# Turning normalised tokens by halves, inside the stage in front, at three seams of a hybrid attention kernel

## The chip, the cores and the metric

One core of one Trainium2 chip runs the whole program. The metric is the device time of one execution in microseconds, lower being better. The profiled execution's span runs from the program's first instruction to its last.

## What is computed

For each of 16 sequences of L = 1024 tokens with D = 256 channels, float32, a block of four residual steps:

```python
x = x + attn_a(layernorm(x))     # delta rule + two causal convolutions + values, mixed by a router, then Wo
x = x + slot_ffn(layernorm(x))   # 64 slots, top-8 routing, a GRU step on the slots, values mixed back
x = x + attn_b(layernorm(x))     # causal softmax attention, 16 heads of 16
x = x + slot_ffn(layernorm(x))
def layernorm(x): return (x - mean(x)) / sqrt(var(x) + 1e-5)      # over the channels
```

The slot step begins with `h = gelu(layernorm(x) @ w1 ...)` and softmax attention with `qkv = layernorm(x) @ w_qkv`. Both need the normalised tokens with the channels on the partitions.

## The kernel before

A hardware loop goes over the 16 sequences; each is a row of stages: convolutions and delta rule, router, mixing (`mix_and_project`), slot step `ffa`, softmax attention (`softmax_attention`), slot step `ffb`. A stage is one or more Blocks. In a Block each engine has a program of its own, in the order in which it is written, and waits for others by semaphores; at a Block's end all five engines meet, and only then does the next Block begin.

The tokens live in SBUF as T = 8 tiles of 128 tokens by 256 channels (`k.x1`, normalised in `k.xn`). PSUM is `ps`, 8 banks of 512 float32 a partition. `k.xnT` holds the normalised tokens turned: 2 halves of the channels (`HALVES`) by 1024 tokens, which are 2 halves of 512 tokens (`NB`, `BANK`). So a turning is 16 transposes of 128x128 on TensorE (PE) into four banks, then two copies by ScalarE (ACT) and two by VectorE (DVE).

A seam is the end of one stage and the beginning of the next. There are three in question: mixing to `ffa` (the mixing seam), `ffa` to softmax attention (the slot seam), and softmax attention to `ffb` (the softmax seam). At each, in front of the Block's end:

- PE projects to the tokens (L1238, L1352, L1769), two tiles to a bank.
- VectorE adds them to `k.x1` and takes the statistics, two tiles at a time (L303, L266 to L272); GpSimd raises to the power -1/2 and makes the shift (L280, L282); ScalarE normalises tile by tile (L287).
- PE, done with its projection, runs 8 matmuls of `keep_warm` (L312), whose results nobody reads.

Behind the Block's end PE turns all 16 (L319), ScalarE copies (L327), VectorE copies (L333), and the next stage's first matmuls follow: L1292 in a slot step, L1804 in softmax attention. They wait for `xn0` and `xn1`, once for each half of the tokens. In the slot step L1399 is VectorE's first instruction on the router's logits; in softmax attention L1618 is the first matmul of scores for the running maximum.

The trace has two records for each float32 matmul that is not a transpose: L1292 is 4 matmuls and 8 records, L1804 16 and 32.

Of the kernel before, what the change touches and what calls it, by code (L numbers as in the profile page):

```python
# [18 lines left out]
ACT = mybir.ActivationFunctionType  # L19
# [4 lines left out]
P = 128  # L24
SEQS, L, D = 16, 1024, 256
T = L // P
HALVES = D // P
# [262 lines left out]

def normalise(nc, k, s, act, x):

    for t in range(T):
        act.wait_ge(s.rstd, 2 * (t // 2 + 1))
        normalise_tile(nc, k, x, t)

# [17 lines left out]

def turn_normed_pe(nc, k, ps, s):
    for n in range(NB):
        for a in range(HALVES):
            for i in range(BANK // P):
                last = nc.tensor.transpose(ps[:, 4 + HALVES * n + a, i * P:(i + 1) * P],  # L319
                                           k.xn[:, n * (BANK // P) + i, a * P:(a + 1) * P], k.ident[:])  # L320
            last.then_inc(s.xn_turned, 1)


def turn_normed_act(nc, k, ps, s, act):
    for n in range(NB):
        act.wait_ge(s.xn_turned, HALVES * n + 1)
        nc.scalar.activation(k.xnT[:, 0, n * BANK:(n + 1) * BANK], ps[:, 4 + HALVES * n, :], ACT.Copy).then_inc(s.xn0, 1)  # L327


def turn_normed_dve(nc, k, ps, s, dve):  # L330
    for n in range(NB):
        dve.wait_ge(s.xn_turned, HALVES * n + 2)
        nc.vector.tensor_copy(k.xnT[:, 1, n * BANK:(n + 1) * BANK], ps[:, 4 + HALVES * n + 1, :]).then_inc(s.xn1, 1)  # L333


def first_norm(nc, k, ps, s, io):

    with nc.Block() as block:
        @block.scalar
        def _(act):  # L340
            for t in range(T):
                act.wait_ge(s.rstd, 2 * (t // 2 + 1))
                normalise_tile(nc, k, k.x0, t).then_inc(s.next_normed, 1)
            turn_normed_act(nc, k, ps, s, act)

        @block.vector
        def _(dve):
            settle = chain_of(dve, s.dve)
            dve.wait_ge(io.loaded, 16)
            for u in range(T // 2):  # L350
                norm_statistics(nc, k, s, settle, k.x0, u)
            turn_normed_dve(nc, k, ps, s, dve)

        @block.gpsimd
        def _(pool):
            inverse_deviations(nc, k, s, pool)

        @block.tensor
        def _(pe):
            pe.wait_ge(s.next_normed, T)  # L360
            turn_normed_pe(nc, k, ps, s)
    clear(nc, s)
# [770 lines left out]
def mix_and_project(nc, k, m, ps, s):  # L1133

    with ExitStack() as tmp:
# [20 lines left out]
        with nc.Block() as block:  # L1156
# [8 lines left out]
            @block.vector  # L1165
            def _(dve):
                settle = chain_of(dve, s.dve)
                for n in range(NB):
                    for i in range(PATHS):
                        nc.vector.tensor_tensor(of(paths[i], n), of(paths[i], n),  # L1170
                                                m.prob[:, n * GN:(n + 1) * GN, i:i + 1].to_broadcast([P, GN, DH]),
                                                ALU.mult).then_inc(s.part, 1)
                for n in range(NB):
                    dve.wait_ge(s.summed, n + 1)
                    nc.vector.tensor_scalar(ms[:, n * GN:(n + 1) * GN], ps[:, SUMS + n, 0:GN], EPS * EPS, None,
                                            ALU.add).then_inc(s.scale_in, 1)
# [5 lines left out]
                add_with_statistics(nc, k, s, dve, settle, lambda u: ps[:, 4 + u, :], base=k.x0)  # L1182

            @block.scalar
            def _(act):
# [10 lines left out]
                normalise(nc, k, s, act, k.x1)  # L1196

            @block.tensor
            def _(pe):
# [52 lines left out]
                project(1)  # L1252
                keep_warm(nc, k, ps[:, 0, :], 8)
    clear(nc, s)
# [7 lines left out]
def slot_ffn(nc, k, ps, s, tag, io=None, store=None, load=None):  # L1262

    with ExitStack() as tmp:
# [19 lines left out]
        with nc.Block() as block:  # L1284
            @block.tensor
            def _(pe):
                turn_normed_pe(nc, k, ps, s)
                for n in range(NB):
                    pe.wait_ge(s.xn0, n + 1)
                    pe.wait_ge(s.xn1, n + 1)  # L1290
                    for c in range(HALVES):
                        last = nc.tensor.matmul(ps[:, n, :], k.w1x[:, c, :], k.xnT[:, c, n * BANK:(n + 1) * BANK],  # L1292
                                                start=(c == 0), stop=(c == HALVES - 1))
                    last.then_inc(s.h_ps, 1)
# [53 lines left out]
                for t in range(T):  # L1348
# [5 lines left out]
                    if t % 2:  # L1354
                        last.then_inc(s.out, 1)
                keep_warm(nc, k, ps[:, 7, :], 8)

            @block.scalar
            def _(act):
                turn_normed_act(nc, k, ps, s, act)  # L1360
                for n in range(NB):
# [29 lines left out]
                if store is None:  # L1391
                    normalise(nc, k, s, act, k.x1)

            @block.vector
            def _(dve):
                settle = chain_of(dve, s.dve)
                turn_normed_dve(nc, k, ps, s, dve)
                dve.wait_ge(s.logits, 1)
# [46 lines left out]
                if store is None:  # L1445
                    add_with_statistics(nc, k, s, dve, settle, lambda u: ps[:, u, :])
                else:
                    for u in range(T // 2):
# [96 lines left out]
def softmax_attention(nc, k, ps, s, stacked, ones_rows):  # L1545

    with ExitStack() as tmp:
# [231 lines left out]
        with nc.Block() as block:  # L1779
# [15 lines left out]
            def _(pe):  # L1795
                turn_normed_pe(nc, k, ps, s)
                for u in range(2 * HALVES * NB):
                    i, a, n = unit(u)
                    pe.wait_ge(s.xn0, n + 1)
                    pe.wait_ge(s.xn1, n + 1)  # L1800
                    if u >= 4:
# [53 lines left out]
                for t in range(BANK // P, T):  # L1855
                    last = project_out_pe(pe, late_slot, t, range(1, HALVES))
                    if t % 2:
                        last.then_inc(s.out, 1)
                keep_warm(nc, k, ps[:, RING_BANK, :], 8)

            @block.scalar
            def _(act):
# [3 lines left out]

                turn_normed_act(nc, k, ps, s, act)
                for u in range(2 * HALVES * NB + 1):
# [17 lines left out]
                nc.scalar.activation(oT[:, 1, BANK:L], ps[:, RING_BANK, :], ACT.Copy).then_inc(s.ot1, 1)  # L1886
                normalise(nc, k, s, act, k.x1)

            @block.vector
            def _(dve):  # L1890
                settle = chain_of(dve, s.dve)
                turn_normed_dve(nc, k, ps, s, dve)
                for u in range(2 * HALVES * NB):
# [26 lines left out]
                for u in (2, 3):  # L1920
                    add_out_dve(dve, settle, late_slot, u)
                    norm_statistics(nc, k, s, settle, k.x1, u)

            @block.sync
# [43 lines left out]

COMMON = "dve var rstd xn_turned xn0 xn1"
SET_OF = {"su": 1, "pc": 2, "dr": 1, "ro": 0, "mi": 1, "ff": 0, "sa": 1}  # L1970
# [163 lines left out]
```

## Time and profile before

| | |
|---|---|
| median of 3 runs | 8637.09 us (8602.2 to 8650.65) |
| profiled execution | 8632.0 us, its span 8630.2 us |
| granted TensorE clock, mean over the span | 0.921 |
| busy: PE, DVE, ACT, POOL | 90%, 56%, 39%, 17% |
| instructions | 126086 |

[...]

### The profile page before, as it was taken

Reading aid. Unit: us, or ns where it says so; the run is one execution under the profiler, and the core shown is the slowest. Engines: PE = TensorE matmul, PEld = TensorE weight load, DVE = VectorE, ACT = ScalarE, POOL = GpSimd, SP = SyncE. Lnnn points to the kernel's source line nnn. Section 1 sums busy time; section 2 is a strip of 40 time slices with the busy share of each in tenths; the row PEclk is TensorE's granted clock in tenths of the full one; section 3 lists DMA queues with packets and bytes.
Section 4 is the critical chain, followed back from the end, with each engine's and each line's share of the span. In section 5 each row is a group of like instructions: output and inputs, shape, how many; then the busy total and the mean of one; then the engine's idle time right before and its main releaser. Section 6 shows DMA issues by size and latency. Waiting matters only on the chain. (4 is left out here: it accounts for less than half of the span.)

```text
span 8630.2 us, 126086 instructions
## 1 busy us (share of the span) xinstructions
PE 7756.3 (90%) x49774; PEld 4709.9 (55%) x49774; DVE 4846.4 (56%) x9442; ACT 3377.0 (39%) x6843; POOL 1453.5 (17%) x2145
## 2 busy tenths in 40 slices
PE   6899998989889899898988988999899998998889
PEld 4546465464554646546465464654646546465464
DVE  5555655556645566555665546555465554656546
ACT  2252533525335243352533425334253342534425
POOL 2102121121211212112121121211212112121111
PEclk9999989989989898999989999899898999989989
DMA  2120111201112021120211102111021110211102
GB/s 70 19 41 17 31 44 23 43 10 31 44 23 43 10 31 44 23 43 10 36 40 29 38 9 36 40 31 45 1 36 40 31 45 1 41 35 31 45 1 40
DMA packets 337658, 268.92 MB, mean 31 GB/s; under 512 B 213377, under 2 KB 276225, under 8 KB 336953
## 3 DMA queue, kind: packets, MB, share of 16 engines
q1 hardware_dynamic: 337004, 260.04, 15.3%
q8 instruction: 430, 7.05, 0.4%
q14 instruction: 224, 1.84, 0.1%
HBM read 48.66 MB, written 42.02 MB: 11 GB/s over the span
## 5 line engine op out<-in xcount | busy, mean ns | idle before, releaser
L1716 ACT ACTIVATE sa_pt<-ps 128x512 f32<-128x512 f32 (+3 forms) x3072 | 1283.4, 492 | 793.7 <-PE ps L1705 639.3
L1637 DVE TENSOR_REDUCE sa_nm<-ps 128x2 f32<-128x1024 f32 (+4 forms) x1280 | 1388.9, 1115 | 341.0 <-PE ps L1618 148.3
L1701 PE MATMUL ps<-sa_qs,sa_ks 99*128 99x512 bf16 (+3 forms) x3072 | 846.3, 332 | 55.8 <-ACT sa_pt L1716 40.3
L1618 PE MATMUL ps<-sa_ks,sa_qs 96*128 96x512 bf16 (+3 forms) x2560 | 629.6, 320 | 50.8 <-DVE sa_nm L1637 32.1
L312 PE MATMUL ps<-identb 128*128 128x512 bf16 x2560 | 647.9, 405 | 10.5 <-ACT dr_z L988 10.5
L1726 PE MATMUL ps<-sa_pt,sa_va 128*17 128x512 f32 (+3 forms) x6144 | 641.8, 491 | 0.0
L1701 PEld LDWEIGHTS ps<-sa_qs,sa_ks 99*128 99x128 bf16 x3072 | 288.2, 98 | 613.3 <-ACT sa_pt L1716 411.6
L576 PE MATMUL ps<-rep,stack 128*32 128x512 f32 x4608 | 501.0, 593 | 0.0
L280 POOL TENSOR_TENSOR rstd<-vare,mhalf 128x2 f32<-128x2 f32 x260 | 181.3, 697 | 1789.8 <-DVE vare L272 1789.8
L312 PEld LDWEIGHTS ps<-identb 128*128 128x128 bf16 x2560 | 259.9, 105 | 316.7 <-issue 77.7
L287 ACT ACTIVATE xn<-x,shift,rstd 128x256 f32<-128x256 f32 x520 | 278.4, 593 | 393.8 <-POOL shift L282 393.4
L797 POOL TENSOR_TENSOR A<-paths 128x256 f32<-128x256 f32 x384 | 269.6, 734 | 866.9 <-DVE paths L954 866.9
L1705 PE MATMUL ps<-causalT,identb 128*128 128x128 bf16 x2048 | 414.3, 221 | 0.0
L678 DVE SCALAR_TENSOR_TENSOR k_tm<-pre,cw,k_tm 128x1024 f32<-128x1024 f32 x192 | 245.3, 1284 | 233.5 <-ACT k_tm L620 228.9
L1618 PEld LDWEIGHTS ps<-sa_ks,sa_qs 96*128 96x128 bf16 x2560 | 241.1, 99 | 223.1 <-DVE sa_nm L1637 61.1
L1622 PE MATMUL ps<-causal,identb 128*128 128x128 bf16 x1792 | 336.3, 220 | 0.0
L576 PEld LDWEIGHTS ps<-rep,stack 128*32 128x32 f32 x4608 | 146.5, 110 | 335.0 <-issue 335.0
L1206 PE MATMUL ps<-ident,paths 128*128 128x128 f32 x2048 | 265.8, 296 | 67.1 <-DVE paths L1170 67.1
L1068 DVE COPY ro_partial<-ps 128x512 f32<-128x512 f32 x32 | 22.1, 692 | 539.3 <-PE ps L1100 539.3
L1658 POOL CAST sa_mp<-sa_nm 128x16 bf16<-128x16 f32 x128 | 25.3, 198 | 1723.8 <-DVE sa_nm L1637 1723.8
L319 PE MATMUL ps<-ident,xn 128*128 128x128 f32 x784 | 148.6, 370 | 169.6 <-PEq L1156 54.9
L1206 PEld LDWEIGHTS ps<-ident,paths 128*128 128x128 f32 x2048 | 260.1, 211 | 68.7 <-DVE paths L1170 68.7
(343 smaller groups left out, 14866.5 us busy)
## 6 DMA issues: line engine op xcount, KB each, us to landing
sa_qs<-sa_parts SPq DMA_DIRECT2D x288, 128.0 KB, 4.4
sa_ks<-sa_parts SPq DMA_DIRECT2D x288, 128.0 KB, 5.7
x<-in_x SPq DMA_DIRECT2D x17, 1024.0 KB, 5.5
rep<-paths SPq DMA_DIRECT2D x128, 128.0 KB, 2.3
bounce<-paths SPq DMA_DIRECT2D x32, 512.0 KB, 2.6
out_y<-x SPq DMA_DIRECT2D x32, 512.0 KB, 3.0
rep<-paths SPq DMA_DIRECT2D x128, 127.9 KB, 2.4
rep<-paths SPq DMA_DIRECT2D x128, 127.8 KB, 2.3
```

Of the source, the lines that this page charges most:

```text
L287: return nc.scalar.activation(k.xn[:, t, 0:D], x[:, t, :], ACT.Identity, bias=k.shift[:, t:t + 1], scale=k.rstd[:, t:t + 1])
L312: nc.tensor.matmul(scratch, k.identb[:, 0:P], k.identb[:], start=True, stop=True)
L576: last = nc.tensor.matmul(ps[CG * g:CG * (g + 1), 4 + u % 4, :], k.stack[:, (base + j) * GROUPS + gg, :], rep[:, gg, PAD + n * BANK - SHIF ...
L797: nc.gpsimd.tensor_tensor(with_delta[:, t % 2, 1 + n, :], m.delta_tm[:, t, :], paths[n][:, t, :], ALU.mult).then_inc(s.d_products, 1)
L1206: last = nc.tensor.matmul(ps[:, HALVES * n + a, j * P:(j + 1) * P], paths[i][:, n * TN + j, a * P:(a + 1) * P], k.ident[:], start=(i == 0 ...
L1618: last = nc.tensor.matmul(cols[:, i, :], qs[0:NCOMB * AD, g % NBUF, op.j + i, op.t * P:(op.t + 1) * P], ks[0:NCOMB * AD, g % NBUF, op.j + ...
L1622: last = nc.tensor.matmul(cols[:, i, op.w - P:], k.identb[:, 0:P], k.causal[:], start=False, stop=True, skip_group_check=True)
L1637: nc.vector.tensor_reduce(nm[:, g % 2, op.c, op.t, op.j:op.j + op.heads], cols, AX.X, ALU.max, negate=True).then_inc(s.slot_free, 1)
L1701: last = nc.tensor.matmul(bank[:, off:], ks[0:QROWS, g % NBUF, j, kt * P:(kt + 1) * P], qs[0:QROWS, g % NBUF, j, n * BANK + off:(n + 1) * ...
L1705: last = nc.tensor.matmul(bank[:, off:off + P], k.identb[:, 0:P], k.causalT[:], start=False, stop=True, skip_group_check=True)
L1716: nc.scalar.activation(pt[:, gs % 2, j, off:BANK], ring_bank(ring_use(gs, j))[:, off:], ACT.Exp, scale=RATIO).then_inc(s.ring_out, 1)
L1726: last = nc.tensor.matmul(ps[2 * AD * j:2 * AD * j + AD + 1, SUM_BANK, off:BANK], va[:, kt, g * GH + j, :], pt[:, gs % 2, j, off:BANK], st ...
```

## The change

The first norm of the program, in front of the loop, is turned by the same new functions. At the three seams the turning moves in front of the Block's end and is cut in two by halves of the tokens: PE waits for tiles 0 to 3, turns them, runs warm-ups (12 in the mixing and slot seams, 10 in the softmax seam, where 8 stood), waits for tiles 4 to 7 and turns them. ScalarE copies its part of the first half behind tile 5 and that of the second behind tile 7; VectorE copies behind its last statistics. The next stage's first matmuls wait for nothing but the Block. Banks of `ps` are given by `first`: 0 to 3 in the mixing seam, 4 to 7 in the others.

```diff
-def normalise(nc, k, s, act, x):
+def normalise_and_turn(nc, k, ps, s, act, first):
     for t in range(T):
         act.wait_ge(s.rstd, 2 * (t // 2 + 1))
-        normalise_tile(nc, k, x, t)
+        normalise_tile(nc, k, k.x1, t).then_inc(s.xn_normed, 1)
+        if t in (T - 3, T - 1):
+            turned_act(nc, k, ps, s, act, first, t // (T - 1))
...
+def turn_pe(nc, k, ps, s, pe, first, n):
+
+    pe.wait_ge(s.xn_normed, (n + 1) * (BANK // P))
+    for a in range(HALVES):
+        for i in range(BANK // P):
+            last = nc.tensor.transpose(ps[:, first + HALVES * n + a, i * P:(i + 1) * P],
+                                       k.xn[:, n * (BANK // P) + i, a * P:(a + 1) * P], k.ident[:])
+        last.then_inc(s.xn_turned, 1)
+
+
+def turned_act(nc, k, ps, s, act, first, n):
+
+    act.wait_ge(s.xn_turned, HALVES * n + 1)
+    nc.scalar.activation(k.xnT[:, 0, n * BANK:(n + 1) * BANK], ps[:, first + HALVES * n, :], ACT.Copy)
+
+
+def turned_dve(nc, k, ps, s, dve, first, n):
+
+    dve.wait_ge(s.xn_turned, HALVES * n + 2)
+    nc.vector.tensor_copy(k.xnT[:, 1, n * BANK:(n + 1) * BANK], ps[:, first + HALVES * n + 1, :])
...
                 project(1)
-                keep_warm(nc, k, ps[:, 0, :], 8)
+                turn_pe(nc, k, ps, s, pe, 0, 0)
+                keep_warm(nc, k, ps[:, 2, :], 12)
+                turn_pe(nc, k, ps, s, pe, 0, 1)
...
-                turn_normed_pe(nc, k, ps, s)
                 for n in range(NB):
-                    pe.wait_ge(s.xn0, n + 1)
-                    pe.wait_ge(s.xn1, n + 1)
...
-                keep_warm(nc, k, ps[:, 7, :], 8)
+                if store is None:
+                    turn_pe(nc, k, ps, s, pe, 4, 0)
+                    keep_warm(nc, k, ps[:, 6, :], 12)
+                    turn_pe(nc, k, ps, s, pe, 4, 1)
+                else:
+                    keep_warm(nc, k, ps[:, 7, :], 8)
...
-                keep_warm(nc, k, ps[:, RING_BANK, :], 8)
+                turn_pe(nc, k, ps, s, pe, RING_BANK, 0)
+                keep_warm(nc, k, ps[:, SUM_BANK, :], 10)
+                turn_pe(nc, k, ps, s, pe, RING_BANK, 1)
```

PE's program at the mixing seam before, with line numbers of the kernel before; `mi_ot` is the mixed output that is projected, L1156 and L1285 are the end of one Block and the beginning of the next:

```order
L1238 MATMUL ps<-wo,mi_ot 128x256 x16
L312 MATMUL ps<-identb 128x512 x8
L1156 UNCONDITIONAL_BRANCH
L1285 UNCONDITIONAL_BRANCH
L319 MATMUL ps<-ident,xn 128x128 x16
L1292 MATMUL ps<-xnT,w1x 128x512 x4
```

And in the changed kernel, with its own line numbers (L1245 is the projection, L322 the turning, L314 the warm-ups, L1298 the slot step's first matmuls):

```order
L1245 MATMUL ps<-wo,mi_ot 128x256 x16
L322 MATMUL ps<-ident,xn 128x128 x8
L314 MATMUL ps<-identb 128x512 x12
L322 MATMUL ps<-ident,xn 128x128 x8
L1161 UNCONDITIONAL_BRANCH
L1294 UNCONDITIONAL_BRANCH
L1298 MATMUL ps<-xnT,w1x 128x512 x4
```

The turning stands in front of the Block's end in two pieces, with the warm-ups between them. At the slot seam PE's program in the changed kernel is this; L1358 gives the slot step's output, L1812 is softmax attention's first matmul:

```order
L1358 MATMUL ps<-ffa_values,ffa_alphat 128x256 x8
L322 MATMUL ps<-ident,xn 128x128 x8
L314 MATMUL ps<-identb 128x512 x12
L322 MATMUL ps<-ident,xn 128x128 x8
L1293 UNCONDITIONAL_BRANCH
L1805 UNCONDITIONAL_BRANCH
L1812 MATMUL ps<-xnT,wqkvT 128x512 x16
```

The last 8 transposes are queued behind all 12 warm-ups. ScalarE's program at the mixing seam in the changed kernel; L287 normalises, L330 is its copy of turned tokens, L1373 the slot step's first activation:

```order
L287 ACTIVATE xn<-x,shift,rstd 128x256 x6
L330 ACTIVATE xnT<-ps 128x512
L287 ACTIVATE xn<-x,shift,rstd 128x256 x2
L330 ACTIVATE xnT<-ps 128x512
L1161 UNCONDITIONAL_BRANCH
L1369 UNCONDITIONAL_BRANCH
L1373 ACT_TABLE_LOAD
```

Before, eight L287 stood in a row in front of the Block's end and both copies behind it; now one copy stands between the sixth and the seventh tile.

## Rows read from the trace of the kernel before

**Rows 1.** The page, first part: busy us, share of the span, instructions.

```profile
PE 7756.3 (90%) x49774; PEld 4709.9 (55%) x49774; DVE 4846.4 (56%) x9442; ACT 3377.0 (39%) x6843; POOL 1453.5 (17%) x2145
```

**Rows 2.** Waits: who waited for whom, us in total, times, longest us.

```profile
PE ps L319 <- PEq L1156: 54.9, 16, 3.4
```

**Rows 3.** Timeline, first mixing seam: start us, us, what [idle before it, its end].

```profile
328.73 1.89 PE L312 MATMUL ps<-identb 128*128 128x512 bf16 x8
328.80 1.09 ACT L287 ACTIVATE xn<-x,shift,rstd 128x256 f32<-128x256 f32 x2 [0.84 <-POOL shift L282]
...
332.66 1.09 ACT L287 ACTIVATE xn<-x,shift,rstd 128x256 f32<-128x256 f32 x2 [0.83 <-POOL shift L282]
...
334.05 3.65 PE L319 MATMUL ps<-ident,xn 128*128 128x128 f32 x16 [3.43 <-PEq L1156]
...
336.02 0.69 DVE L333 COPY xnT<-ps 128x512 f32<-128x512 f32 x1 [4.45 <-PE ps L319]
...
337.49 4.87 PE L1292 MATMUL ps<-xnT,w1x 128*128 128x512 f32 x8
...
344.28 0.69 DVE L1399 TENSOR_TENSOR ffa_lg<-ps,b 128x512 f32<-128x512 f32 x1 [5.86 <-PE ps L1297]
```

**Rows 4.** Timeline, first softmax seam.

```profile
551.17 2.06 ACT L287 ACTIVATE xn<-x,shift,rstd 128x256 f32<-128x256 f32 x4
...
554.61 2.13 PE L312 MATMUL ps<-identb 128*128 128x512 bf16 x8
...
559.58 1.94 PE L319 MATMUL ps<-ident,xn 128*128 128x128 f32 x16 [2.84 <-PEq L1779]
...
560.68 0.69 DVE L333 COPY xnT<-ps 128x512 f32<-128x512 f32 x1 [3.57 <-PE ps L319]
...
561.52 3.67 PE L1292 MATMUL ps<-xnT,w1x 128*128 128x512 f32 x8
```

**Rows 5.** Mixing seams, 16 stretches: A:B, us, busy us (instructions), PEclk, DMA.

```profile
333.75:344.28 10.53, 10.23 (x41) 7.34 (x42) 1.38 (x3) 5.04 (x7) 0.00 (x0) 0.70 0.00 0
...
8362.67:8370.50 7.83, 7.53 (x41) 5.26 (x42) 1.38 (x2) 5.04 (x7) 0.00 (x0) 1.00 0.00 0
sum 158.79, PE 154.07 PEld 112.64 DVE 22.16 ACT 80.54 POOL 0.00; mean PE 9.63 PEld 7.04 DVE 1.39 ACT 5.03 POOL 0.00
```

**Rows 6.** Slot seams, 16 stretches, columns as in rows 5.

```profile
378.32:394.54 16.22, 15.91 (x49) 7.73 (x49) 6.23 (x9) 8.49 (x16) 6.61 (x7) 1.00 0.16 54
...
8404.14:8422.43 18.29, 17.98 (x49) 9.66 (x49) 6.23 (x9) 8.49 (x16) 6.61 (x7) 0.86 0.14 48
sum 272.05, PE 267.19 PEld 135.29 DVE 99.61 ACT 135.85 POOL 105.62; mean PE 16.70 PEld 8.46 DVE 6.23 ACT 8.49 POOL 6.60
```

**Rows 7.** Softmax seams, 16 stretches, columns as in rows 5.

```profile
559.29:567.11 7.82, 7.53 (x41) 5.26 (x42) 1.39 (x2) 5.03 (x6) 0.00 (x0) 1.00 0.43 135
1093.58:1102.84 9.26, 8.97 (x41) 6.63 (x42) 1.39 (x3) 5.03 (x6) 0.00 (x0) 0.82 0.36 113
...
sum 142.03, PE 137.34 PEld 101.63 DVE 22.16 ACT 80.48 POOL 0.00; mean PE 8.58 PEld 6.35 DVE 1.38 ACT 5.03 POOL 0.00
```

**Rows 8.** Timeline, first slot seam, then the last sequence's.

```profile
366.75 6.65 PE L1352 MATMUL ps<-ffa_values,ffa_alphat 64*128 64x256 f32 x16 [0.51 <-DVE ffa_values L1444]
...
373.33 3.60 PE L312 MATMUL ps<-identb 128*128 128x512 bf16 x8
...
380.56 13.97 PE L1804 MATMUL ps<-xnT,wqkvT 128*128 128x512 f32 x32
...
8396.62 1.90 PE L312 MATMUL ps<-identb 128*128 128x512 bf16 x8
...
8404.44 3.65 PE L319 MATMUL ps<-ident,xn 128*128 128x128 f32 x16 [5.91 <-PEq L1284]
```

**Rows 9.** Stretches of the first slot seam, columns as in rows 5.

```profile
367.40:377.50 10.10, 9.53 (x23) 5.20 (x21) 7.42 (x28) 3.55 (x7) 3.57 (x8) 0.50 0.00 0
377.70:394.54 16.84, 15.91 (x49) 7.73 (x49) 6.23 (x9) 9.11 (x17) 6.61 (x7) 1.00 0.15 52
```

More of the change, by code:

```diff
@@ L312, in keep_warm @@
         nc.tensor.matmul(scratch, k.identb[:, 0:P], k.identb[:], start=True, stop=True)
[L315 to L333, printed above, removed]
+def turn_pe(nc, k, ps, s, pe, first, n):
[11 more added lines that the diff above has]
+    nc.vector.tensor_copy(k.xnT[:, 1, n * BANK:(n + 1) * BANK], ps[:, first + HALVES * n + 1, :])
 def first_norm(nc, k, ps, s, io):
@@ L342, in _ @@
                 act.wait_ge(s.rstd, 2 * (t // 2 + 1))
-                normalise_tile(nc, k, k.x0, t).then_inc(s.next_normed, 1)
-            turn_normed_act(nc, k, ps, s, act)
+                normalise_tile(nc, k, k.x0, t).then_inc(s.xn_normed, 1)
+            for n in range(NB):
+                turned_act(nc, k, ps, s, act, 4, n)
         @block.vector
@@ L351, in _ @@
                 norm_statistics(nc, k, s, settle, k.x0, u)
-            turn_normed_dve(nc, k, ps, s, dve)
+            for n in range(NB):
+                turned_dve(nc, k, ps, s, dve, 4, n)
         @block.gpsimd
@@ L359, in _ @@
         def _(pe):
-            pe.wait_ge(s.next_normed, T)
-            turn_normed_pe(nc, k, ps, s)
+            for n in range(NB):
+                turn_pe(nc, k, ps, s, pe, 4, n)
     clear(nc, s)
@@ L1182, in _ @@
                 add_with_statistics(nc, k, s, dve, settle, lambda u: ps[:, 4 + u, :], base=k.x0)
+                for n in range(NB):
+                    turned_dve(nc, k, ps, s, dve, 0, n)
             @block.scalar
@@ L1195, in _ @@
                     nc.scalar.activation(of(wide, n), bc(scale[:, n * GN:(n + 1) * GN], DH), ACT.Copy).then_inc(s.wide, 1)
-                normalise(nc, k, s, act, k.x1)
+                normalise_and_turn(nc, k, ps, s, act, 0)
             @block.tensor
@@ L1286, in _ @@
             def _(pe):
-                turn_normed_pe(nc, k, ps, s)
                 for n in range(NB):
-                    pe.wait_ge(s.xn0, n + 1)
-                    pe.wait_ge(s.xn1, n + 1)
                     for c in range(HALVES):
@@ L1355, in _ @@
                         last.then_inc(s.out, 1)
-                keep_warm(nc, k, ps[:, 7, :], 8)
+                if store is None:
[4 more added lines that the diff above has]
+                    keep_warm(nc, k, ps[:, 7, :], 8)
             @block.scalar
             def _(act):
-                turn_normed_act(nc, k, ps, s, act)
                 for n in range(NB):
@@ L1391, in _ @@
                 if store is None:
-                    normalise(nc, k, s, act, k.x1)
+                    normalise_and_turn(nc, k, ps, s, act, 4)
             @block.vector
@@ L1396, in _ @@
                 settle = chain_of(dve, s.dve)
-                turn_normed_dve(nc, k, ps, s, dve)
                 dve.wait_ge(s.logits, 1)
@@ L1446, in _ @@
                     add_with_statistics(nc, k, s, dve, settle, lambda u: ps[:, u, :])
+                    for n in range(NB):
+                        turned_dve(nc, k, ps, s, dve, 4, n)
                 else:
@@ L1795, in _ @@
             def _(pe):
-                turn_normed_pe(nc, k, ps, s)
                 for u in range(2 * HALVES * NB):
                     i, a, n = unit(u)
-                    pe.wait_ge(s.xn0, n + 1)
-                    pe.wait_ge(s.xn1, n + 1)
                     if u >= 4:
@@ L1865, in part @@
                     return parts[i][:, which, a, n * BANK:(n + 1) * BANK]
-                turn_normed_act(nc, k, ps, s, act)
                 for u in range(2 * HALVES * NB + 1):
@@ L1886, in _ @@
                 nc.scalar.activation(oT[:, 1, BANK:L], ps[:, RING_BANK, :], ACT.Copy).then_inc(s.ot1, 1)
-                normalise(nc, k, s, act, k.x1)
+                normalise_and_turn(nc, k, ps, s, act, RING_BANK)
             @block.vector
@@ L1891, in _ @@
                 settle = chain_of(dve, s.dve)
-                turn_normed_dve(nc, k, ps, s, dve)
                 for u in range(2 * HALVES * NB):
@@ L1922, in _ @@
                     norm_statistics(nc, k, s, settle, k.x1, u)
+                for n in range(NB):
+                    turned_dve(nc, k, ps, s, dve, RING_BANK, n)
             @block.sync
@@ L1963, in softmax_attention @@
         clear(nc, s)
-COMMON = "dve var rstd xn_turned xn0 xn1"
+COMMON = "dve var rstd xn_normed xn_turned"
 SET_OF = {"su": 1, "pc": 2, "dr": 1, "ro": 0, "mi": 1, "ff": 0, "sa": 1}
```

## The prediction

> **What bounds the kernel now.** I read the page's first part first. [...] Then I looked for the idle time in front of the turning matmuls of line 319. It is not small change: in the mixing seams alone PE stands idle for 54.9 us over 16 times, 3.4 us each, released by the end of a Block [rows 2]. So at a seam PE does not set the pace at first: the chain there is VectorE's statistics, GpSimd's power, ScalarE's normalising (one pair of tiles each 1.93 us, the last pair ends at 333.75), then the turning, the two copies, and the next stage's first matmuls.
>
> The timeline of the first mixing seam [rows 3] is to be read as follows. PE's 8 warm-ups end at 330.6 and nothing runs until the turning at 334.05, 0.29 after the last normalising ends at 333.75. The 16 transposes run at half speed (3.65 for what takes 1.94 in [rows 4]), and so do the next stage's first matmuls (L1292, first to start at 337.49). The first instruction of VectorE in the slot stage proper, L1399, starts at 344.28. At the first softmax seam [rows 4] the same work runs at the full clock: last normalising to L1292 is 2.23 (559.29 to 561.52).
>
> To see how often each happens I cut three stretches from each of the 16 sequences: from the end of the last normalising to L1399 in the mixing seam and in the softmax seam, and to the first L1618 in the slot seam. With their granted clock these say:
> - mixing seam [rows 5]: 10.5 us ten times, 9.0 to 9.2 five times, 7.83 once, at a granted clock of 0.70, 0.81 and 1.00. The sum is 158.79.
> - slot seam [rows 6]: 16.2 us ten times at 1.00, 18.3 six times at 0.86. The sum is 272.05.
> - softmax seam [rows 7]: 7.82 four times at 1.00, about 9.2 twelve times at 0.82. The sum is 142.03.
>
> So the three stretches hold 573 us of the 8632.0 of the profiled execution, and what differs in them is the clock alone.
>
> **The change part by part.** At each seam it takes the 16 transposes, ScalarE's two copies and VectorE's two copies from behind the Block's end to the front of it; the first 8 transposes wait for four normalised tiles only, the last 8 for eight. It adds warm-ups: 12 for 8 in the mixing and slot seams, 10 for 8 in the softmax seam, and these now stand between the two halves. It removes the waits on xn0 and xn1. What is not moved: ScalarE gets its first copy of 0.6 between the third pair of tiles and the fourth, where it now waits 0.83 for GpSimd's shift [rows 3]; so that copy costs nothing, and would cost 0.6 if that cover were gone. VectorE's first copy comes after its last statistics, when it has nothing until the turning is done. The DMA queues: SP's only moved step is the load of the next x0 at the softmax seam, which begins with the Block and so some 2 us later; its first reader on VectorE stands behind the whole routing that L1399 begins; nothing.
>
> *At the full clock* the new seam is: last normalising to PE 0.06 (chosen; it lies between nothing and the 0.29 that a whole Block end takes), 1.10 until VectorE can start (559.58 to 560.68 [rows 4], that is 8 transposes and their landing), copy 0.69, Block end 0.29, together 2.14 against 2.23. That is 0.09 a seam: the gain of half a turning is eaten by the copy, which lay beside the next stage's matmuls or the second half before and now lies ahead of the Block's end. *At the half clock* it is 0.06 + 1.97 (334.05 to 336.02 [rows 3]) + 0.69 + 0.29 = 3.01 against 3.74, so 0.73. The change is therefore about the clock, and each seam has its own answer.
>
> *Mixing seam.* Before, PE idles 3.4 us and the clock is low when it starts again, in 15 of 16. Now projection ends about 328.7 (the warm-ups follow it there), four tiles are ready at 329.89 [rows 3], 8 transposes take 0.87 and 12 warm-ups at 0.21 take 2.6, to about 333.4; the last 8 start at 333.81 and end at 334.7, and the next stage's matmul comes at 335.9. PE's pauses are then 1.2, 0.4 and 1.2 us, in place of one of 3.4. The clock was at full ahead of the seam (8 warm-ups in 1.89), and in [rows 4] PE pauses 2.84 after its warm-ups and the turning still runs at full. I expect full clock all 16 times: 2.14 + 5.59 (561.52 to 567.11) = 7.73, times 16 = 123.7, against 158.8: **-35 us**.
>
> *Slot seam.* Here the new place of the warm-ups costs. In the ten sequences like [rows 8, 9] the value matmuls (L1352) already run at half clock, and the clock is at 0.50 up to 377.5 and at 1.00 from 377.7. Four tiles are ready at 374.45, two periods of 1.93 before the last normalising ends at 378.32 [rows 6]; 8 transposes at half clock take 8 x 0.213 = 1.7, to 376.2; of the 12 warm-ups 3.2 are done at 0.43 by 377.6, the other 8.8 take 1.9, to 379.5. The last 8 transposes, which could start at 378.38, stand behind them in PE's queue: the stage begins at 379.5 + 2.08 = 381.6 instead of 380.56 [rows 8], +1.0. In the six at 18.3 PE reached the turning at half clock (8404.44 [rows 8]) after two pauses; now it pauses 3.7 (from the 8396.6 at which L1352 ends to 8400.3), likely drops too, and comes back during the warm-ups: I take 17.6, -0.7. Together 10.0 - 4.2 = **+6 us**. The bounds: every time full and in time, 16 x 16.13 = 258, -14; every time 12 warm-ups at the half clock, 374.51 + 1.71 + 5.12 = 381.34, then 1.97 + 0.69 + 0.29, so 5.96 after the last normalising instead of 2.23, 16 x 19.95 = 319, +47.
>
> *Softmax seam.* The late projection ends 4.7 before the last normalising (554.6 [rows 4]); four tiles are long ready (553.2), so the first turning and the 10 warm-ups run at once, 0.87 + 2.1, and end some 2 us before the last tile. Then come 8 transposes, 0.9, then a pause of 1.2. That is a long thin stretch, where before 16 transposes and the 8 records of L1292 ran without a break. I expect a mix: a third at 7.7, a third at the 9.2 of today, a third at the 10.5 that the mixing seam shows when the clock stays low through L1292. The mean is 9.3 to 9.4 against 8.88: **+8 us**. The bounds: 123.7 (-18) and 16 x 10.53 = 168 (+26).
>
> Sum: -35 + 6 + 8 = -21. The profiled execution took 8632.0, the median of three 8637.09; the same step from the median gives **8616 us**.
>
> **The rivals.**
> A, the forecast: mixing seam freed, part of it given back. Chance 0.50.
> B, all three seams stay at full clock: -35 - 14 - 18 = -67, 8570 us. For it: the warm-ups now fill the pause. Against it: in ten slot seams the clock is low before the changed part begins. 0.18.
> C, slower: in the slot seam the 12 warm-ups delay the last 8 transposes at the half clock. At its full price, with the softmax seam at 10.5: -35 + 47 + 26 = +38, 8675 us. It decides from the point where slot and softmax seams together lose more than the mixing seam's 2.2 us a sequence. For it: the clock of 0.50 in [rows 9]. Against it: it returns by 377.6 there, with as much work before it as after. 0.12.
> D, the change does nothing: the clock falls in the mixing seam all the same, because PE's work there is now in three pieces with pauses between. Then a mixing seam saves 0.73 fifteen times, 11 us, and the losses of 14 elsewhere stay: +3, 8640 us. For it: at [rows 5] 9.2 appears as well as 10.5, so a small shift changes the outcome. Against it: the pauses are all shorter than the one that goes. 0.20.
>
> [...]
>
> **How the numbers follow.** 0.5%, about 43 us, is what I take a measurement of this kernel to tell from no change; the three runs of before lie 48 us apart. Faster by over that needs under 8594: B and the lower edge of A, 0.20. Slower by over that needs above 8680: only C at more than its full price, 0.04. Within: 0.76. The range 8585 to 8655 takes in A and D with the spread of the clock's luck, leaves out most of B (0.13) and the upper half of C (0.07).
>
> **What would show it.** In the profile after, the mixing stretch should sum to 124 (each 7.7, clock 1.00), the slot stretch to 278 with single ones of 17 to 18 and the warm-ups' last ends behind the last normalising, the softmax stretch to 150 with its granted clock between 0.7 and 1.00. Last normalising to first next matmul should be 2.14 at full clock. Wrong would be: 9 us or more in mixing stretches (D), slot stretches of 19 and more (C), slot and softmax at 16.1 and 7.7 throughout (B), or a change outside the three seams, whose 8059 us I take as untouched.

## The result, and the profile after

| | before | after |
|---|---|---|
| median, 20 runs each on one chip | 8641.39 us | 8605.11 us (8545.94 to 8662.99) |
| ratio, 95% interval | 1 | 0.9951 (0.9936 to 0.9967) |
| profiled execution, its span | 8632.0, 8630.2 us | 8612.26, 8610.4 us |
| granted clock, mean over the span | 0.921 | 0.929 |

The granted clock is the share of TensorE's full clock that the profile records. In each of the fourteen profiles every one of its 308 to 394 records is 0.5 or 1.0, here the half clock and the full one; a figure between the two is the mean over a stretch that has both. The first mixing seam's 8 warm-ups took 1.89 us [rows 3], where before's granted clock is 1.00, the first slot seam's 3.60 [rows 8] at 0.50 [rows 9].

The change makes the kernel 0.5% faster: 36 us between the medians, 42 us (28 to 55) by the ratio. The forecast was 8616 with a range of 8585 to 8655.

The first part of the page of after. PE has 160 more instructions than in [rows 1] and is busy 13 us less, which fits its higher clock:

```profile
PE 7743.1 (90%) x49934; PEld 4689.0 (54%) x49934; DVE 4844.8 (56%) x9442; ACT 3369.1 (39%) x6843; POOL 1452.1 (17%) x2145
```

In after's lines the turning is L322, the warm-ups L314, the copies L330 (ScalarE) and L336 (VectorE), the value matmuls L1358, and the next stage's first matmuls L1298 (slot step) and L1812 (softmax attention). The timeline of after's first mixing seam, the rows that answer to [rows 3]; the columns are as there:

```profile
335.52 1.09 PE L322 MATMUL ps<-ident,xn 128*128 128x128 f32 x8 [1.05 <-ACT xn L287]
...
336.45 2.75 PE L314 MATMUL ps<-identb 128*128 128x512 bf16 x12
...
338.24 1.09 ACT L287 ACTIVATE xn<-x,shift,rstd 128x256 f32<-128x256 f32 x2 [0.36 <-POOL shift L282]
...
339.38 1.09 PE L322 MATMUL ps<-ident,xn 128*128 128x128 f32 x8 [0.18 <-ACT xn L287]
...
340.51 0.69 DVE L336 COPY xnT<-ps 128x512 f32<-128x512 f32 x1 [2.77 <-PE ps L322]
...
341.50 3.67 PE L1298 MATMUL ps<-xnT,w1x 128*128 128x512 f32 x8 [1.03 <-PEq L1161]
```

The 3.43 us in which PE stood still has become 1.05, 0.18 and 1.03. The 8 records of L1298 take 3.67 instead of 4.87, the full-clock figure of [rows 4]. From the last normalising (ends 339.33) to L1298 is 2.17, where the prediction had 2.14. ScalarE's last gap in front of its normalising shrank from 0.83 to 0.36, because its first copy is inside it: that copy cost nothing.

The same stretches as in [rows 5 to 7], of after. First the mixing seams:

```profile
339.33:347.10 7.77, 6.69 (x33) 4.39 (x34) 0.69 (x2) 4.43 (x5) 0.00 (x0) 1.00 0.00 0
...
sum 124.31, PE 106.97 PEld 70.22 DVE 11.08 ACT 70.92 POOL 0.00; mean PE 6.69 PEld 4.39 DVE 0.69 ACT 4.43 POOL 0.00
```

The slot seams:

```profile
381.69:400.09 18.40, 17.33 (x48) 7.73 (x46) 5.54 (x8) 7.88 (x14) 6.62 (x7) 0.96 0.14 47
916.29:933.63 17.34, 16.29 (x48) 7.42 (x46) 5.53 (x8) 7.88 (x14) 6.61 (x7) 1.00 0.15 50
...
sum 282.66, PE 265.94 PEld 119.90 DVE 88.53 ACT 126.14 POOL 105.62; mean PE 16.62 PEld 7.49 DVE 5.53 ACT 7.88 POOL 6.60
```

The softmax seams:

```profile
566.75:574.52 7.77, 6.69 (x33) 4.39 (x34) 0.69 (x1) 4.43 (x5) 0.00 (x0) 1.00 0.45 136
...
1637.72:1646.91 9.19, 8.11 (x33) 4.98 (x34) 0.69 (x1) 4.43 (x5) 0.00 (x0) 0.81 0.37 114
...
6976.35:6987.15 10.80, 9.71 (x33) 5.47 (x34) 0.69 (x2) 4.43 (x5) 0.00 (x0) 0.68 0.31 97
...
sum 138.93, PE 121.59 PEld 76.12 DVE 11.08 ACT 70.92 POOL 0.00; mean PE 7.60 PEld 4.76 DVE 0.69 ACT 4.43 POOL 0.00
```

Of the mixing stretches all sixteen are at 1.00. Of the slot stretches ten are at 1.00 and 17.1 to 17.3 us, six at 0.94 to 0.96 and 18.4 to 18.7. Of the softmax stretches nine are at 1.00, four at 0.81 to 0.82, three at 0.68. The sums moved by -34.5, +10.6 and -3.1, together -27.0 (from 572.9 to 545.9).

### The profile page after: what moved, and what is told of

It reads as the page before. It is cut to its first block and busy times, and to the rows that moved or that the text cites. A ratio compares the mean times of both kernels' runs of the same rounds, so it can differ in the third digit from the quotient of the medians.

```text
span 8610.4 us, 126198 instructions
## 1 busy us (share of the span) xinstructions
PE 7743.1 (90%) x49934; PEld 4689.0 (54%) x49934; DVE 4844.8 (56%) x9442; ACT 3369.1 (39%) x6843; POOL 1452.1 (17%) x2145
## 5 line engine op out<-in xcount | busy, mean ns | idle before, releaser
L314 PE MATMUL ps<-identb 128*128 128x512 bf16 x2720 | 677.6, 401 | 10.5 <-ACT dr_z L993 10.5
L314 PEld LDWEIGHTS ps<-identb 128*128 128x128 bf16 x2720 | 278.5, 105 | 323.7 <-issue 69.1
L287 ACT ACTIVATE xn<-x,shift,rstd 128x256 f32<-128x256 f32 x520 | 278.2, 592 | 378.3 <-POOL shift L282 377.9
L396 DVE TENSOR_TENSOR paths<-paths 128x31 f32<-128x31 f32 (+15 forms) x496 | 170.4, 343 | 208.6 <-DMA paths<-bounce 192.1
```

The source lines that it names most:

```text
L287: return nc.scalar.activation(k.xn[:, t, 0:D], x[:, t, :], ACT.Identity, bias=k.shift[:, t:t + 1], scale=k.rstd[:, t:t + 1])
L314: nc.tensor.matmul(scratch, k.identb[:, 0:P], k.identb[:], start=True, stop=True)
```

## The experiments

My theory: at the mixing seam PE's pause of 3.4 us lets the clock fall (in before's first one the granted clock is 1.00 up to 333.22, inside the pause, and 0.50 from there to 340.05), and what the change does there is to break the pause up; the shorter way from the last normalising to the next matmul is worth almost nothing. The rivals: the new order itself saves the time; the warm-ups alone do it wherever the turning stands; the slot and softmax seams take part with a sign of their own. Each kernel is read by two things, its ratio to before and the sums of the three groups of stretches in its profile. In before the pause in front of the turning is 3.4 in all sixteen mixing seams, yet ten stretches take 10.5, five 9.0 to 9.2 and one, at full clock throughout, 7.83; what decides between these is not shown. A sum comes from one profiled execution; how far it moves by itself is seen from the second profiles of before and after, in the last two rows of the table. In every experiment the very first norm, in front of the loop, is turned as in after:

| kernel | runs | ratio (95% interval) | mixing | slot | softmax | all |
|---|---|---|---|---|---|---|
| before | 20 | 1 | 158.8 | 272.1 | 142.0 | 572.9 |
| after | 20 | 0.9951 (0.9936 to 0.9967) | 124.3 | 282.7 | 138.9 | 545.9 |
| mixing_alone | 12 | 0.9967 (0.9948 to 0.9987) | 124.3 | 289.3 | 133.9 | 547.5 |
| slot_alone | 12 | 1.0002 (0.9978 to 1.0026) | 155.5 | 285.6 | 136.4 | 577.5 |
| softmax_alone | 12 | 0.9982 (0.9961 to 1.0003) | 158.6 | 272.9 | 142.7 | 574.2 |
| filled_not_moved | 12 | 0.9977 (0.9954 to 1.0000) | 125.2 | 290.3 | 132.3 | 547.8 |
| mixing_no_warm | 10 | 1.0014 (0.9984 to 1.0044) | 169.7 | 284.1 | 147.8 | 601.7 |
| slot_no_warm | 10 | 0.9987 (0.9968 to 1.0005) | 124.3 | 313.0 | 146.2 | 583.5 |
| slot_4_and_8 | 4 | 0.9918 (0.9898 to 0.9937) | 124.3 | 263.7 | 149.0 | 537.0 |
| softmax_14 | 6 | 0.9940 (0.9918 to 0.9962) | 124.3 | 288.3 | 125.6 | 538.2 |
| combined | 8 | 0.9905 (0.9872 to 0.9938) | 124.4 | 262.5 | 124.7 | 511.6 |
| filled_at_all_three | 7 | 0.9912 (0.9879 to 0.9946) | 125.2 | 274.6 | 128.7 | 528.5 |
| before_again | 1 | none, 8655.65 us | 150.5 | 283.1 | 142.4 | 576.0 |
| after_again | 1 | none, 8600.43 us | 124.4 | 283.4 | 144.0 | 551.7 |

In the experiments' own lines the turning in front of a Block's end is L327, the warm-ups L319, the turning behind it L355, the normalising L292, the value matmuls L1405, the next stage's first matmuls L1345 and L1872.

### One seam at a time

Each kernel is before with one seam changed as in after, the other two left. The core of the edit for the mixing seam, with the copies moved to match; the other two are done in the same way:

```diff
-                keep_warm(nc, k, ps[:, 0, :], 8)
+                turn_pe(nc, k, ps, s, pe, 0, 0)
+                keep_warm(nc, k, ps[:, 2, :], 12)
+                turn_pe(nc, k, ps, s, pe, 0, 1)
```

**mixing_alone.** 

> The change at the mixing seam alone, the slot and softmax seams as before. Theory of the clock (TensorE no longer falls to half clock at this seam): the 16 mixing stretches sum to 124 us (7.77 each, clock 1.00), the others stay near 272 and 142 or shift with the clock's luck by up to 10, the time falls by 35, ratio 0.996. Rival, the gain is the turning's shorter way (0.73 at half clock, 0.09 at full) and the clock does what it did: mixing stretches sum to 148, ratio 0.999.

**slot_alone.** 

> The change at the slot seam alone, 12 warm-ups between the halves. Theory: the warm-ups hold up the last 8 transposes, the 16 slot stretches sum to 280 to 285 us against 272.05, ratio 1.001. Rival, the seam is a gain of its own and the losses seen come from what the mixing seam does to the clock: the sum is under 265, ratio 0.999.

**softmax_alone.** 

> The change at the softmax seam alone. Theory: stretches of 7.8, 9.2 and 10.6 side by side, sum 135 to 145 us against 142.03, time the same within 0.1%. Rival, this seam gives the rest of the measured gain that the mixing seam does not explain: sum under 128, ratio 0.998.

The mixing seam alone gives 124.3 in its own stretches and a ratio of 0.9967, most of what the whole change gives. The other two alone can't be told from no change. But the sums are not additive. With the mixing seam freed and the slot seam untouched, the slot stretches take 289.3, more than the shift of up to 10 that I had allowed for: twelve of sixteen are at a clock of 0.83 to 0.86, where before it was six. The two sums alone don't show that the seams are coupled, since before_again, with no edit at all, has 283.1. What shows it is the pairing of the stretches of one sequence. In [rows 5] and [rows 6] the first sequence has 10.53 and then 16.22, the last 7.83 and then 18.29. The fourth has this:

```profile
1944.11:1953.30 9.19, 8.90 (x41) 6.84 (x42) 1.38 (x2) 5.03 (x6) 0.00 (x0) 0.81 0.00 0
1986.94:2005.30 18.36, 18.05 (x49) 9.66 (x49) 6.23 (x9) 8.49 (x16) 6.61 (x7) 0.86 0.14 48
```

Before, before_again and softmax_alone have both seams as before, 48 pairs in all. Of these 27 mixing stretches took about 10.5, and the slot stretch behind them 16.2 in 25 and 18.9 in two. The other 21 took 9.2 or less, and the slot stretch behind them 18.2 to 18.4 every time. The clock at the value matmuls that lie between (from 11.5 to 6 us ahead of the last normalising) was 0.54 to 0.56 in all 27 and 1.00 in all 21. So a mixing stretch of 10.5 goes with value matmuls at the half clock and, mostly, a slot stretch at full clock; a shorter one goes with the reverse. With every mixing stretch freed (mixing_alone and filled_not_moved) 22 of 32 value matmuls ran at 1.00, and the slot stretches behind them took 18.3 to 18.7; behind the other ten they took 16.2 seven times and 18.9 three times. What carries the clock's state from the one seam to the value matmuls was not followed.

The pairing also gives the price of the moved turning at the slot seam. In slot_alone the first two slot stretches stand behind mixing stretches of 10.53 and 9.01:

```profile
380.27:397.57 17.30, 16.24 (x48) 7.36 (x46) 5.54 (x8) 7.89 (x15) 6.63 (x7) 1.00 0.15 51
907.11:925.50 18.39, 17.24 (x47) 7.74 (x47) 5.54 (x8) 7.89 (x14) 6.62 (x7) 0.96 0.14 48
```

All eight behind 10.5 took 17.2 to 17.3 (16.2 without the move), all eight behind 9.2 or less 18.4 to 18.5 (18.2 to 18.4 without it): about 1.1 us in the first kind, 0.1 in the second. That is some 9 of the 13.5 between 285.6 and 272.1; the rest comes from two more sequences of the dear kind. Beside a freed mixing seam the moved slot seam took 282.7, 283.4 and 288.3 (after, after_again, softmax_14), the unmoved one 289.3 and 290.3 (mixing_alone, filled_not_moved), so there the move costs nothing that shows and may save a little.

### Warm-ups without the move

filled_not_moved is before with one number changed at the seams:

```diff
-                keep_warm(nc, k, ps[:, 0, :], 8)
+                keep_warm(nc, k, ps[:, 0, :], 21)
```

> The kernel before with one change: 21 warm-ups in place of 8 at the mixing seam, in front of the Block's end, nothing moved. They end some 0.5 us before the last normalising. Theory of the clock: the fall to half clock goes away without any moving, the 16 mixing stretches sum to 125 us (7.83 each), ratio 0.996, the same as the moved seam. Rival, moving is what gains: the sum stays at 140 to 159, ratio 0.999 to 1.000.

Its first mixing stretch and the sum, columns as in [rows 5]:

```profile
343.97:351.79 7.82, 7.49 (x40) 5.26 (x42) 1.38 (x2) 5.03 (x6) 0.00 (x0) 1.00 0.00 0
...
sum 125.19, PE 119.88 PEld 84.18 DVE 22.14 ACT 80.48 POOL 0.00; mean PE 7.49 PEld 5.26 DVE 1.38 ACT 5.03 POOL 0.00
```

And the end of that seam in its timeline:

```profile
339.17 4.48 PE L319 MATMUL ps<-identb 128*128 128x512 bf16 x20
...
344.26 1.94 PE L355 MATMUL ps<-ident,xn 128*128 128x128 f32 x16 [0.61 <-PEq L1194]
```

All sixteen turnings stay behind the Block's end, 16 in a row, and the stretch is at full clock all the same: 0.61 us of pause in place of 3.43 (one record of the 21 is missing from the trace). Of the 34.5 us in the mixing stretches 33.6 come without moving anything. The rest, 0.9 over 16 seams, is what the order is worth there: 0.06 a seam, where I had worked out 0.09. The measured ratio is weaker evidence: 0.9977, with an interval that reaches 1.0000 and overlaps those of after and mixing_alone, so it neither proves a gain in time by itself nor sets the kernel apart from after.

### The move without warm-ups

mixing_no_warm is after with no warm-ups at the mixing seam:

```diff
                 turn_pe(nc, k, ps, s, pe, 0, 0)
-                keep_warm(nc, k, ps[:, 2, :], 12)
                 turn_pe(nc, k, ps, s, pe, 0, 1)
```

> The changed kernel without the 12 warm-ups at the mixing seam; the turning stays moved and halved. Theory of the clock: TensorE pauses 2.9 us between the halves, falls to half clock around the last 8 transposes in most sequences, and the mixing stretches sum to 145 to 170 us instead of 124.3. Rival, the moved turning alone is the gain: the sum stays at 124 to 130.

The two turnings in its first mixing seam, then the stretches:

```profile
345.03 1.09 PE L327 MATMUL ps<-ident,xn 128*128 128x128 f32 x8 [1.05 <-ACT xn L292]
...
348.89 1.97 PE L327 MATMUL ps<-ident,xn 128*128 128x128 f32 x8 [2.77 <-ACT xn L292]
```

```profile
348.84:360.41 11.57, 10.49 (x33) 6.16 (x34) 0.69 (x2) 4.44 (x6) 0.00 (x0) 0.61 0.00 0
...
sum 169.73, PE 152.38 PEld 93.38 DVE 11.09 ACT 70.94 POOL 0.00; mean PE 9.52 PEld 5.84 DVE 0.69 ACT 4.43 POOL 0.00
```

The first eight take 1.09, the full clock; behind a pause of 2.77 the next eight take 1.97, the half clock. The seam is then worse than before's (169.7 against 158.8), though the turning stands where after has it. So both halves of the question have an answer in the mixing stretches: the warm-ups without the move give the gain, and the move without them loses 11 us against the first profile of before (19 against the second). Its ratio, 1.0014, can't be told from 1; from after's 0.9951 it is well apart.

slot_no_warm takes the 12 warm-ups out of the slot seam of after in the same way.

> The changed kernel without the 12 warm-ups at the slot seam. Theory, the warm-ups hold up the last 8 transposes: last normalising to the first L1812 (the stage's first matmul) falls from 3.68 us on average to 2.2 to 3.0, but nothing lifts the clock, so that L1812 runs longer at half clock and the slot stretches sum to 290 to 310 us against 282.66. Rival, the hold-up is the whole of the loss: the sum falls to 265 to 272.

The last normalising to the next stage's first matmul is 3.05 on the mean instead of 3.68 (2.79 in before), since nothing stands in PE's queue in front of the last eight transposes. But the stretches go to 313.0, a little above what was expected: the clock now stays low through the first part of L1872 (0.50 up to 386.65 in the first seam, 5.7 us into it), whose 32 records take 16.82 there where they take 13.97 at the full clock [rows 8]. The delay by the warm-ups was real, and the clock was worth more than it. The ratio, 0.9987 (0.9968 to 1.0005), puts the kernel just behind after, whose interval ends at 0.9967.

### Where the warm-ups stand at the slot seam

The timeline of after's first slot seam shows the delay. First PE's value matmuls and the first eight transposes, then 12 warm-ups, then the last eight transposes, and between them the normalising that those wait for:

```profile
369.57 7.19 PE L1358 MATMUL ps<-ffa_values,ffa_alphat 64*128 64x256 f32 x16 [0.51 <-DVE ffa_values L1453]
...
377.87 1.97 PE L322 MATMUL ps<-ident,xn 128*128 128x128 f32 x8 [1.11 <-ACT xn L287]
...
379.63 4.54 PE L314 MATMUL ps<-identb 128*128 128x512 bf16 x12
...
380.59 1.09 ACT L287 ACTIVATE xn<-x,shift,rstd 128x256 f32<-128x256 f32 x2 [0.36 <-POOL shift L282]
...
384.02 1.04 PE L322 MATMUL ps<-ident,xn 128*128 128x128 f32 x8
386.08 2.38 PE L1812 MATMUL ps<-xnT,wqkvT 128*128 128x512 f32 x5 [1.03 <-PEq L1293]
```

The last tiles are ready at 381.68; the transposes start at 384.02, because the warm-ups ran at the half clock until 383.25:

```profile
376.80:382.90 6.10, 5.03 (x16) 2.91 (x17) 3.23 (x13) 3.69 (x7) 1.78 (x4) 0.50 0.00 0
383.10:399.00 15.90, 14.87 (x43) 7.04 (x42) 4.84 (x7) 7.39 (x14) 6.09 (x6) 1.00 0.15 49
```

slot_4_and_8 is after with fewer warm-ups behind the first eight transposes and some in front:

```diff
+                    keep_warm(nc, k, ps[:, 6, :], 4)
                     turn_pe(nc, k, ps, s, pe, 4, 0)
-                    keep_warm(nc, k, ps[:, 6, :], 12)
+                    keep_warm(nc, k, ps[:, 6, :], 8)
                     turn_pe(nc, k, ps, s, pe, 4, 1)
```

> The changed kernel with the 12 warm-ups of the slot seam placed as 4 ahead of the first 8 transposes and 8 between the halves. Theory: fewer stand in front of the last 8 transposes, and the pause of 3.7 us after the value matmuls is cut, so last normalising to first L1812 falls to 2.5 to 2.9 us on average and the slot stretches sum to 260 to 268 us. Rival, the clock at this seam is set ahead of it and the place of the warm-ups is indifferent: 278 to 285.

```profile
916.45:932.86 16.41, 15.35 (x44) 6.95 (x42) 5.53 (x8) 7.88 (x15) 6.62 (x7) 1.00 0.16 53
...
sum 263.69, PE 246.52 PEld 112.31 DVE 88.55 ACT 126.14 POOL 105.92; mean PE 15.41 PEld 7.02 DVE 5.53 ACT 7.88 POOL 6.62
```

That is its second slot stretch and the sum: 19 us less than after in this seam, with the same 12 warm-ups in all. Fifteen of sixteen are at 1.00 and between 16.2 and 16.7 us. The ratio is 0.9918 (0.9898 to 0.9937), better than after's 0.9951 (0.9936 to 0.9967); it rests on four runs, and the two intervals just touch. The softmax stretches of the same profile, whose code is after's, are at 149.0: 10 more than in after's profile. Whether that is a coupling or the spread of one profile, this run doesn't tell; the same code has 144.0 in after_again.

### Four more warm-ups at the softmax seam

```diff
-                keep_warm(nc, k, ps[:, SUM_BANK, :], 10)
+                keep_warm(nc, k, ps[:, SUM_BANK, :], 14)
```

> The changed kernel with 14 warm-ups in place of 10 at the softmax seam. Theory: with 10 PE is done 2 us too early and the clock falls in about half the sequences; 14 close the pause and the softmax stretches sum to 124 to 130 us against 138.94. Rival, the clock falls for want of work behind the last normalising (8 transposes in 2.2 us): the sum stays at 135 to 142.

All sixteen softmax stretches of softmax_14 are at 1.00 and between 7.8 and 8.2, 125.6 in all against 138.9 in after. The ratio, 0.9940 (0.9918 to 0.9962), is on the right side of after's 0.9951, but the intervals overlap. The two that take 8.2 are those in which the 14 end 0.7 us after the last normalising, the latest of all, so 14 is about the most that fits there.

### Both together, and the fair comparison

combined is after with both edits. filled_at_all_three is before with 21, 20 and 20 warm-ups at the three seams for 8 each, and nothing moved:

```diff
-                keep_warm(nc, k, ps[:, RING_BANK, :], 8)
+                keep_warm(nc, k, ps[:, RING_BANK, :], 20)
```

**combined.** 

> The changed kernel with both mended places: 4 warm-ups ahead and 8 between the halves at the slot seam, 14 between them at the softmax seam, the mixing seam as changed. Theory: the gains add, the stretches sum to 124 (mixing), 264 (slot) and 126 to 130 (softmax), 514 to 518 us together against 545.9 of the changed kernel and 572.9 of the one before; the time falls by 55 to 60 from the kernel before, ratio 0.993. Rival, a gain at one seam sets the clock worse at the next, as the mixing seam did to the slot seam: together 530 or more, ratio 0.995.

**filled_at_all_three.** 

> The kernel before with nothing moved and more warm-ups in front of the three Blocks' ends: 21 at the mixing seam, 20 at the slot seam, 20 at the softmax seam, where 8 stood. Theory, the clock is nearly all of it: mixing 125, softmax 125 to 130, slot 262 to 275 us, 512 to 530 together, ratio 0.993 to 0.995. Rival, splitting the turning is needed for the slot and softmax seams: slot 285 or more or softmax 135 or more, ratio 0.996 and above.

The first slot seam in the timeline of combined, to set beside after's above:

```profile
363.21 1.04 PE L319 MATMUL ps<-identb 128*128 128x512 bf16 x4
...
366.92 1.97 PE L327 MATMUL ps<-ident,xn 128*128 128x128 f32 x8 [2.67 <-ACT xn L292]
...
368.68 2.42 PE L319 MATMUL ps<-identb 128*128 128x512 bf16 x8
...
370.93 1.04 PE L327 MATMUL ps<-ident,xn 128*128 128x128 f32 x8
...
373.00 2.38 PE L1872 MATMUL ps<-xnT,wqkvT 128*128 128x512 f32 x5 [1.03 <-PEq L1334]
```

The clock falls in the pause of 2.67, at 366.32, and is back at 369.74, before the eight warm-ups end (2.42 us for eight, which take 1.89 at the full clock [rows 3] and 3.60 at the half [rows 8]). The last transposes start 0.20 behind the last normalising (370.73), and L1872 follows 2.27 behind it. The three sums of combined are 124.4, 262.5 and 124.7, at 0.9905 of before's time (median 8545.45; by the two ratios 0.5% below after). This is the lowest ratio of the study, though its interval, 0.9872 to 0.9938, takes in the ratios of slot_4_and_8 and filled_at_all_three. The three sums come to 511.6, a little below the 514 to 518 expected, so here the gains did add. filled_at_all_three reaches 0.9912 (0.9879 to 0.9946) with nothing moved; the intervals of after and of this kernel overlap a little, so that it is faster than the studied change is likely but not settled. Its interval and combined's overlap almost wholly, so a measured gain of the move over well-filled seams isn't shown; in the stretches it is 17 us (528.5 to 511.6), 12 of them at the slot seam, where 20 warm-ups at the half clock run past the last normalising (seven stretches of 17.4 to 17.9, with six to nine more matmuls in them than the others have).

### How steady one profile is

before_again and after_again are the two kernels unchanged.

**before_again.** 

> The kernel before once more, for a second profile. Theory: its three stretches repeat (mixing 155 to 160, slot 270 to 275, softmax 140 to 144 us) and what lies outside them moves by tens of us from one execution to the next: 8057 in the first profile, 8020 to 8090 now. Rival, the outside is steady within 10 us, so that its difference between kernels would be an effect of the change.

**after_again.** 

> The changed kernel once more, for a second profile. Theory: mixing 124.3 again to 0.1; slot 280 to 290 and softmax 135 to 150 us, since these depend on where the clock's changes fall; outside the stretches 8020 to 8090 against 8064.5. Rival, slot and softmax repeat within 2 us and the outside within 10.

The mixing stretches of after are 124.4 again, sixteen times at 1.00. Before has 150.5 in place of 158.8 there and 283.1 in place of 272.1 at the slot seam; the softmax stretches of after are 144.0 in place of 138.9. For before two of the three expectations missed, mixing at 155 to 160 and slot at 270 to 275, and they missed together: this time six mixing stretches took about 10.5 instead of ten, and by the pairing above more short mixing stretches mean more slot stretches of 18.3. A sum of a seam in which the clock is not settled is good to some 10 us, and a seam that is settled to 0.1. All three together moved from 572.9 to 576.0 for before and from 545.9 to 551.7 for after.

## Why the prediction was right

**Seam by seam.** The mixing term was -35 and is -34.5: sixteen stretches of 7.77 where 7.73 was worked out. The pauses are 1.05, 0.18 and 1.03 where it had 1.2, 0.4 and 1.2, and with them the mixing seam was at 1.00 throughout. Behind a pause of 2.77 the trace of mixing_no_warm shows the half clock (8 transposes in 1.97 us); behind one of 2.84 the trace of before shows the full one (16 in 1.94 [rows 4]). So rival D, the change that does nothing, fell by its own mark, mixing stretches of 9 us or more.

The slot term was +6 and is +10.6 from the first profiles, 0.3 from the second. The mechanism is the one that the prediction describes, warm-ups at the half clock in PE's queue ahead of the last eight transposes; the delay was put at 1.0. From the last normalising to the first matmul it is 3.1 to 3.4 ten times and 4.4 to 4.8 six times, where before it was 2.23 ten times and 3.73 six times: 3.68 on the mean against 2.79. The single stretches came out at 17.1 to 18.7, as "17 to 18" had it. What was wrong is the base: the prediction took before's 272, ten sequences of one kind and six of the other, as what the slot seam would be without the move, and beside a freed mixing seam it is 289 to 290. It treated the seams as independent, and they are not, as the sixteen pairs behind its own [rows 5] and [rows 6] would have shown. That +6 came out near +10.6 is therefore luck in part: a rise of 17 that it did not foresee, less the 7 by which the moved seam stayed below the unmoved one, where it had a cost of 6 for the move. Rival C, the slot seam late at its full price, stayed out: none reached 19.

The softmax term was +8 and is -3.1 (+1.6 between the second profiles, 142.4 to 144.0). The mix of full, 9.2 and 10.8 is there, but in nine, four and three parts, not in thirds. The prediction's own sum is off here too: a third each at 7.7, 9.2 and 10.5 has a mean of 9.1, not 9.3 to 9.4, so its mix was worth +4 and not +8, and the total by it -25. This is the term with the wrong size; the code of that seam gave 138.9, 144.0 and 149.0 in after, after_again and slot_4_and_8, and 146.2 and 147.8 in slot_no_warm and mixing_no_warm, so no single number would have been right to better than 5.

Rival B, all three at the full clock and 67 us, was not what this change reached: 545.9 against the 506 that it stands for. combined comes to 511.6.

**The sum.** -21 was forecast, the stretches give -27 and -24, the measurement -36 between medians and -28 to -55 by the interval. What lies outside the three stretches took 8057.3 and 8077.9 in the two profiles of before, 8064.5 and 8046.9 in those of after, and between 7997.3 and 8075.6 in the other kernels, whose code there differs from before's only in the warm-ups and the first half of the turning ahead of the last normalising. Most of this spread lies between the softmax seam and the next mixing seam, where fifteen stretches sum to between 4440 and 4506. So the 10 us or so between the stretches and the measurement can't be assigned: a small effect of the change on the clock elsewhere and no effect at all are both open. In ten of the eleven kernels other than before the ratio gives more saved, or less lost, than the three sums do (82 against 61 us in combined, 71 against 36 in slot_4_and_8), which speaks for some effect elsewhere but doesn't show it. The prediction's "8059 us I take as untouched" is right as to the instructions and can't be tested closer than some 20 us.

The range held since the mixing term, the one large term, was right in mechanism and size, while the two uncertain ones were small with opposite errors (+5 and -11), which is luck.

## What to carry to other kernels

Where TensorE waits at the end of each stage, cut the trace into stretches from the last result before the wait to the first that depends on it, and read the granted clock of each: here a pause of 3.43 us stood ahead of one mixing stretch of 7.83 at 1.00 and of ten of 10.5 at 0.70, so that it cost mostly by what the clock did behind it. Fill it with matmuls that end just before the awaited data, not after (in the first slot seam of after they ended late and the next stage began 4.40 behind the last normalising, in that of combined 2.27); try this with the order unchanged before the work is moved, since one changed number gave 33.6 of the 34.5 us in the mixing stretches here, and three changed numbers a ratio of 0.9912. A fix at one seam can shift the clock at the next (with both seams as before, slot stretches took 16.2 behind 25 of 27 mixing stretches of 10.5, and 18.2 to 18.4 behind all 21 shorter ones), so pair the stretches of one sequence before you call two seams independent, tune the seams together and compare whole kernels, not one seam at a time.

## What the runs showed of the hardware that I had not expected

PE that was busy didn't always get its clock back. The 16 value matmuls of the first slot seam, on 64 rows instead of 128, ran for 7.19 us with pauses of nothing between them and the clock was 0.50 at their end as at their start:

```profile
369.60:376.70 7.10, 7.10 (x16) 5.13 (x16) 4.77 (x17) 1.09 (x2) 1.78 (x4) 0.50 0.00 0
```

In the same kernel the clock was back at 1.00 at 383.25, during the 12 warm-ups on 128 rows (379.63 to 384.17). Whether the rows, the operands' type or the place makes the difference was not tried. In other sequences the same value matmuls ran at 1.00 from end to end, in 3.72 us in the last one of before.

The second: the slot stretches of slot_4_and_8 end at the full clock whichever way the value matmuls in front of them ran. In the seven microseconds that end 5 us ahead of the last normalising its clock was 0.52 to 0.59 in seven sequences and 1.00 in nine, and fifteen of the sixteen stretches are at 1.00 nevertheless. The place of twelve warm-ups decided more than the clock at which the seam was entered.
